# Summing the keys of the self attention before the row-sum matmuls

## The reference, cut to what matters

```
def sdpa(q, k, v, causal):
    scale = 1.0 / np.sqrt(q.shape[-1])
    scores = jnp.einsum('bhqd,bhkd->bhqk', q * scale, k)
    if causal:
        mask = jnp.tril(jnp.ones((q.shape[-2], k.shape[-2]), dtype=bool))
        scores = jnp.where(mask, scores, jnp.finfo(jnp.float32).min)
    p = jax.nn.softmax(scores.astype(jnp.float32), axis=-1).astype(q.dtype)
    return jnp.einsum('bhqk,bhkd->bhqd', p, v)
```

## Time and profile before

| | us |
|---|---|
| median of 3 runs | 748.28 |
| the three runs | 746.57, 749.37, 748.28 |
| the profiled execution | 751.68 |
| its span | 749.9 |
| PE busy, of the span | 678.5 (90%) |
| DVE busy | 400.0 (53%) |
| ACT busy | 352.7 (47%) |
| POOL busy | 109.0 (15%) |

### The profile page before, as it was taken

How to read it: one execution, slowest core, us unless ns; L and a number is a source line. 1 busy time by engine, 2 the same in 40 slices (tenths; PEclk the granted TensorE clock), 3 DMA queues, 4 the chain that set the end, 5 groups by cost and what they waited for, 6 DMA issues and landing times.

```text
span 749.9 us, 13217 instructions
## 1 busy us (share of the span) xinstructions
PE 678.5 (90%) x5514; PEld 538.6 (72%) x5514; DVE 400.0 (53%) x805; ACT 352.7 (47%) x711; POOL 109.0 (15%) x140
## 2 busy tenths in 40 slices
PE   5997997879999999999889979979799989999995
PEld 4885765548897777778768767755598967776984
DVE  2739537555574555341455684383685374645315
ACT  4522452477352666553434225526473236575424
POOL 0100000480000332200001000007600004132000
PEclk9997999698999999999989969968899999999998
DMA  8132001022004000050400200000120400000000
GB/s 291 64 152 85 2 1 30 1 78 78 1 1 169 1 2 1 1 190 1 183 28 1 77 9 2 2 29 12 68 78 1 168 1 2 1 2 1 0 1 28
DMA packets 6843, 34.54 MB, mean 46 GB/s; under 512 B 1537, under 2 KB 3073, under 8 KB 5249
## 3 DMA queue, kind: packets, MB, share of 16 engines
q1 hardware_dynamic: 5344, 26.85, 9.7%
q10 hardware_dynamic: 1440, 6.86, 2.5%
HBM read 32.66 MB, written 1.05 MB: 45 GB/s over the span
## 4 chain that ended last, share of the span: by engine, by line
PE 75%; DVE 14%; ACT 7%; issue 2%; DMA 1%; POOL 1%; SPq 0%; DVEq 0%; ACTq 0%; POOLq 0%
PE ps_A L733 5%; PE ps_B L952 4%; PE ps_A L952 4%; PE ps_B L733 3%; PE ps_A L915 3%; PE ps_B L915 3%; PE ps_A L1029 3%; PE ps_B L1029 3%; PE ps_B L1079 2%; PE ps_A L1079 2%; PE ps_A L748 2%; PE ps_A L1108 2%; PE ps_B L748 2%; PE ps_A L1067 2%; PE ps_B L863 2%
## 5 line engine op out<-in xcount | busy, mean ns | idle before, releaser
L562 POOL TENSOR_TENSOR xv_A<-big_A 128x256 f32<-128x256 f32 x24 | 18.0, 756 | 215.8 <-ACT big_A L1386 113.6
L562 POOL TENSOR_TENSOR xv_B<-big_B 128x256 f32<-128x256 f32 x24 | 18.5, 776 | 205.2 <-ACT big_B L1386 102.8
L1726 DVE TENSOR_REDUCE max_B<-ps_B 128x2 f32<-128x512 f32 x64 | 40.4, 685 | 14.7 <-PE ps_B L878 9.7
L1726 DVE TENSOR_REDUCE max_A<-ps_A 128x2 f32<-128x512 f32 x64 | 40.0, 685 | 13.9 <-PE ps_A L878 7.2
L1203 ACT ACT_TABLE_LOAD x31 | 39.8, 1283 | 0.5
L733 PE MATMUL ps_A<-q_A,kz_A 128*128 128x256 f32 x264 | 36.8, 300 | 3.2 <-DVE q_A L1617 3.2
L733 PEld LDWEIGHTS ps_A<-q_A,kz_A 128*128 128x128 f32 x264 | 34.7, 203 | 4.9 <-DVE q_A L1617 3.4
L733 PE MATMUL ps_B<-q_B,kz_B 128*128 128x256 f32 x264 | 36.7, 299 | 1.1 <-DVE kz_B L1638 1.1
L733 PEld LDWEIGHTS ps_B<-q_B,kz_B 128*128 128x128 f32 x264 | 34.7, 203 | 2.7 <-issue 2.4
L915 PE MATMUL ps_A<-q_A,kz_A 64*128 64x256 f32 (+1 forms) x320 | 32.7, 317 | 3.7 <-ACT big_A L1390 2.2
L1390 ACT ACTIVATE big_B<-ps_B 128x384 f32<-128x384 f32 (+1 forms) x48 | 23.7, 543 | 23.8 <-PE ps_B L926 23.7
(11 more groups left out here) (413 smaller groups left out, 1651.5 us busy)
## 6 DMA issues: line engine op xcount, KB each, us to landing
ffn_w<-in_l1m SPq DMA_DIRECT2D x2, 3072.0 KB, 11.1
ffn_w<-in_l2f SPq DMA_DIRECT2D x2, 3072.0 KB, 10.3
attn_w<-in_l1a SPq DMA_DIRECT2D x2, 2048.0 KB, 9.2
v_B<-in_l1d ACTq DMA_DIRECT2D x2, 1408.0 KB, 6.8
v_A<-in_l1d ACTq DMA_DIRECT2D x2, 1408.0 KB, 6.4
attn_w<-in_l2q SPq DMA_DIRECT2D x2, 1024.0 KB, 5.1
attn_w<-in_l2q SPq DMA_DIRECT2D x4, 512.0 KB, 4.9
v_A<-in_gm SPq DMA_DIRECT2D x2, 512.0 KB, 5.8
```

Of the source, the lines that this page charges most:

```text
L562: nc.gpsimd.tensor_tensor(L.key_sums(a, i), p[:, 0:S], p[:, S:2 * S], ALU.add)\
L1726: last = nc.vector.tensor_reduce(mx[:, :, h], L.ps[:, h % 4, :].rearrange("p (q k) -> p q k", q=ST), AX.X, ALU.max)
```

## The change

POOL gets a fourth block of additions, for the self heads. It adds the kt = 1 weights of queries 128 to 255 to the kt = 0 weights of the same queries, over 128 columns, and writes the sum into the head's unused first 128 columns. PE then takes the sums of a self head as two matmuls of 128 columns: the kt = 0 weights for queries 0 to 127, and the added tile for queries 128 to 255. That is 256 columns where there were 384. The number of matmuls and weight loads stays the same. Between the values and the sums of a self turn PE now waits on `halves_added`, and the semaphore's count per pass rises from 32 to 48.

All four `ORDER` lists are new. The parts that concern the self attention, read from the lists (sc n is `scores(n)`, W n is `weigh(n)`, what stands in brackets belongs to the other lane):

- PE, the last turn W3 before: lane B, it 0: sc 14, [turn_max], W3. Lane A, it 0: sc 14, [two cross maxima], W3. Lane A, it 1: sc 14, [sc 0], W3. Lane B, it 1: sc 14, [cross queries], W3.
- PE, the last turn W3 after: lane B, it 0: sc 14, [turn_max, sc 0], W3. Lane A, it 0: sc 14, [two cross maxima], W3. Lane A, it 1: sc 14, [sc 4, W0], W3. Lane B, it 1: sc 14, [two steps of self dense], W3.
- POOL after: 16 self adds of B then 16 of A in it 0; 12 of A, 2 of B, 2 of A, 2 of B, 2 of A, 12 of B in it 1. The clearing of both lanes' value buffers (line 571) stands ahead of them in both passes.
- The order of the two lanes also changes in the cross attention of both batches, in the second latent block of it 0, in the second gated memory layer of it 0 and the first of it 1 (lane B now goes first), and in the experts' part of it 1. ACT starts lane B's load of the down weights later (behind lane A's first cross exponentials).

```
 ORDER = {
     "PE": [
         0, 1, 2, 1, 1, 1, 2, 3, 2, 1, 1, 2, 4, 2, 3, 8, 5, 1, 2, 1, 1, 5, 1, 3, 1, 1, 1, 1, 2, 1, 2, 3, 2,
-        3, 1, 3, 1, 2, 1, 1, 1, 4, 2, 1, 2, 1, 1, 1, 1, 2, 2, 1, 1, 2, 2, 2, 5, 1, 1, 1, 1, 1, 1, 1, 2, 2,
+        3, 1, 3, 2, 2, 1, 5, 3, 1, 3, 1, 2, 1, 1, 2, 2, 2, 5, 2, 1, 2, 1, 1, 1, 1, 2, 1, 1, 1, 1, 1, 2, 2,
...
     "POOL": [
-        0, 1, 1, 1, 1, 16, 16, 8, 8, 9, 10, 1, 13, 1, 1, 1, 2, 14, 6, 2, 2, 6, 8, 8],
+        1, 2, 1, 16, 16, 13, 2, 1, 4, 1, 4, 1, 6, 8, 8, 8, 1, 1, 8, 1, 13, 2, 2, 2, 2, 12, 9, 1, 1, 2, 1, 1,
+        3, 4, 2, 8, 6, 2, 2, 6, 8, 8],
...
-                self.halves_added = s("halves_added", 32)
+                self.halves_added = s("halves_added", 48)
...
-                        nc.gpsimd.tensor_tensor(L.key_sums(a, i), p[:, 0:S], p[:, S:2 * S], ALU.add)\
-                            .then_inc(L.halves_added.sem, 1)
+                        if a == SELF:
+                            add = nc.gpsimd.tensor_tensor(p[:, 0:P], p[:, P:S], p[:, S + P:2 * S], ALU.add)
+                        else:
+                            add = nc.gpsimd.tensor_tensor(L.key_sums(a, i), p[:, 0:S], p[:, S:2 * S], ALU.add)
+                        add.then_inc(L.halves_added.sem, 1)
                         yield
...
-                for block in (1, 2, 3):
+                for block in range(4):
                     yield from add_halves(L, block)
...
-                        for part in range(2 if a == SELF else 1):
-                            for kt in range(ST):
-                                lo = kt * P if a == SELF else 0
-                                for j in range(tiles):
-                                    h = order[b * tiles + j]
-                                    at = (1 - kt) * S
-                                    last = mm(strip(j, part, lo), sums(a, h) if part else L.values(a, h, kt),
-                                              L.weights(a, b * tiles + j)[:, at + lo:at + S],
-                                              start=(first and part == 0 and kt == 0),
-                                              stop=(a == SELF and final and part == 1 and kt == ST - 1),
-                                              skip_group_check=True)
-                        if a != SELF:
-                            pe.wait_ge(*L.halves_added.at(it, n0 - HEADS + (b + 1) * tiles))
+                        for kt in range(ST):
+                            lo = kt * P if a == SELF else 0
                             for j in range(tiles):
-                                last = mm(strip(j, 1, 0), sums(a, order[b * tiles + j]), L.key_sums(a, b * tiles + j),
-                                          start=False, stop=final, skip_group_check=True)
+                                at = (1 - kt) * S
+                                mm(strip(j, 0, lo), L.values(a, order[b * tiles + j], kt),
+                                   L.weights(a, b * tiles + j)[:, at + lo:at + S],
+                                   start=(first and kt == 0), stop=False, skip_group_check=True)
+                        pe.wait_ge(*L.halves_added.at(it, n0 + (b + 1) * tiles))
+                        for half in range(2 if a == SELF else 1):
+                            for j in range(tiles):
+                                i = b * tiles + j
+                                if a == SELF:
+                                    p = L.weights(a, i)[:, 0:P] if half else L.weights(a, i)[:, S:S + P]
+                                else:
+                                    p = L.key_sums(a, i)
+                                last = mm(strip(j, 1, half * P)[:, 0:P] if a == SELF else strip(j, 1, 0), sums(a, order[i]), p,
+                                          start=False, stop=(final and half == (a == SELF)), skip_group_check=True)
                         last.then_inc(L.pv_done.sem, 1)
```

## The result

The change made the kernel slower: 752.28 us (median of 9 runs, 751.78 to 754.63) against 746.57 (9 runs of before beside them, 745.11 to 750.00). The ratio is 1.0072, 95% interval 1.0049 to 1.0096, so +5.4 us on 747. The profiled execution took 754.63, its span is 752.8, 2.9 us more than the span before. Both executions were long ones for their kernel: 754.63 is the longest of the nine, and the 751.68 of before is longer than all nine beside it.

A forecast was written before the change was run, and what follows sets the result against it. The prediction took PE to bound the kernel (busy 678.5 of 749.9 us). The profiled 751.68 us, less 3.4, plus 0.9, with wait and order at 0, gave 749.2, or 745.8 on the median's level; range 740 to 752.

The forecast's parts named there:

- What bounds the kernel: Whole kernel: PE, busy 678.5 of 749.9 us and 75% of the chain, sets the pace, also in the self stages.
- the shorter sums on PE: Self attention turns: sums take 0.44 instead of 0.65 us, 0.21 saved in each of 16 turns, 3.4 us in all.
- The added wait: PE between values and sums of a self turn: adds of 0.41 us finish in time, cost 0, at worst 1.2 us.
- 64 adds on POOL: Self stages: POOL's adds hidden, but they meet 14 DVE operations and cost 0.9 us, between 0 and 5.7.
- Rival D: Self stage: POOL and DVE lock each other out and adds come late, +6.1 us, giving 754.4; chance 0.16.
- The new order of steps: Outside the self stage: neighbouring steps of the two lanes exchanged, cost taken as 0, bounds -4.4 to +4.4 us.
- Rival C: Stages behind the self attention wait for DVE's maxima, so the end doesn't see the saving: 748.3 us; chance 0.14.
- Rival B: Cross stages: the new order also cuts PE's idle time by a fifth, 22 to under 19 us, giving 741.4; chance 0.22.
- The signs named for a wrong forecast: Self stages not shorter, or more than 3 us arising or vanishing in stages that compute the same as before.

The follow-up runs named there:

- e1: The edit (self adds, PE's wait, shorter sums) with all steps in the order of before: 745.50 us, ratio 0.9972 to the kernel before.
- e4: Kernel before, old order, with two sums of 128 columns per self head but no adds and no wait: 749.21 us, ratio 0.9989.
- e3: Kernel before, old order, with POOL's self adds and PE's wait, but sums still over 384 columns: 749.84 us, ratio 1.0002.
- e2: Kernel before with the new order of steps on all engines and without the edit: 761.41 us, ratio 1.0169.
- e13: e6 plus the new order in the second half of it 0's latent attention and its feed-forward: 746.81 us, ratio 0.9962 to before.
- e9: e6 plus the new order in the first part of it 0's latent attention: 745.78 us, ratio 0.9955 to before.
- e6: The edit in the order of before, except it 0's start up to lane B's cross scores 12 in the new order: 744.88 us, ratio 0.9943 to before.
- e11: The changed kernel with the end of it 0's cross attention put back to the old order: 752.32 us, ratio 1.0045 to before.
- e10: e6 with lane B's last cross turn, dense and sum of squares of it 0 later on PE, ACT's B steps too: 756.60 us, ratio 1.0112 to before.
- e8: The edit in the order of before, except from lane A's second cross maximum of it 1 to the end, new: 753.30 us, ratio 1.0068 to before.
- e7: The edit in the order of before, except B's eighth up-projection (it 0) to A's second cross maximum (it 1), new: 756.07 us, ratio 1.0110 to before.
- e15: The changed kernel with the gated stages and projections between the iterations put back to the old order: 755.66 us, ratio 1.0100 to before.
- e12: The changed kernel with it 0's cross end and everything from A's second cross maximum of it 1 put back to old: 751.36 us, ratio 1.0040 to before.

## Why the prediction was wrong

*What bounds the kernel, and the shorter sums on PE: right.* A turn on the chain is 1.23 us, as forecast, and the self stage of it 0 is 66.5 - 64.8 = 1.7 us shorter in e1 and e4. That is 8 turns at 0.21, half of the 3.4. (In the new order the whole edit is worth 1.0%, over which part of the lost clock falls too; no term of the sum has that.)

*The added wait: right at 0.* The add was mis-sized, 0.457 and not 0.41 us: a line through two clearings gave POOL's fixed part as 0.10 us, while the two adds (0.727 for 256 columns, 0.457 for 128) make it 0.19. Nothing waited for it all the same.

*64 adds on POOL: 0.9 us forecast, not seen.* e3 has all the adds and the wait and none of the saving, and its ratio is 1.0002. Three adds and one DVE operation of the self stages were stretched, where the term had 14 meetings at a chance of 0.3 each. Rival D had the sign of the result and nearly the size (754.4), by luck: its mechanism did not happen.

*The new order of steps: this is the step that failed.* "Its cost isn't in any row ... a fifth of it won or lost, -4.4 to +4.4. I take 0." The order costs 12.6 us without the edit (e2) and 7.5 us with it, so both the value and the bound were wrong. It accounts for nearly all of the miss: -2.5 was forecast and +5.4 measured, 7.9 us apart. The bound was worked out from PE's idle time in the cross stages, as if the order could only fill or widen those gaps. It left out two things. First, the gated stages, where PE is busy for about 10 of 15 us and the two lanes were swapped (2.0 us with the self stage behind them). Second, the clock. Whole stretches are at 1.2 GHz, and a bound on idle time doesn't hold for what they cost. One lies at 172 to 179 us in the changed kernel, behind the gaps of 3.37 and 1.64 on PE, as if the gaps had brought it on. But e13, with the old cross end and no gap over 1.1 us there, has a stretch of the same length, with PE busy throughout (first row e13; then the changed kernel):

```profile
165.00:172.00 7.00, 7.00 (x40) 6.11 (x32) 1.45 (x2) 1.09 (x2) 3.45 (x4) 0.51 0.01 2
172.00:179.00 7.00, 5.61 (x27) 5.61 (x28) 6.85 (x11) 1.86 (x5) 0.00 (x0) 0.52 0.01 2
```

Before and e9 have it too, e6 and e11 don't. So it is not shown that the new order's gaps bring on slow stretches.

Part of the material for a signed estimate was there. The lists said that B's last cross turn of it 0 moved behind twelve more of A's heads, and the trace of before had the length of the chain from that turn to the up-projection. A look at what fills PE during that chain would have given the sign. It would hardly have given the size: with that look in hand I expected 3 to 5 us of e10, and it was 16.

*Rival C* (the end doesn't see the saving) is half true for single executions: e1 gains 1.7 us in the self stage, and in its profiled execution loses it to the clock right behind. Over 12 runs 2.5 us remain. *Rival B* is wrong for the cross stages (28.5 us idle, not under 19). But some of the new order gains: the start, with A's first scores ahead of B's last self turn, gives another 1.7 us in the self stage (63.1 against 64.8).

The signs named for a wrong forecast held: "if more than 3 us arise or vanish in stages that compute the same as before".

What stays open is what decides between the two lengths of the slow clock with the same steps (e1 and e8, e7 and e8), and so how the 7.5 us divide between the order itself and the clock. Estimates can be had where stages have the same lost clock in two traces. The start is -1.7 us (e6 against e1) and the latent stage -1.6 (e13 against e6). The cross end of it 0 is about +2.6: 90.8 in the changed kernel and e15, against 88.0 and 88.3 in e9 and e13, all with 11.9 lost; the other half of the 5 us between the changed kernel and e11 goes with the clock, 11.9 against 8.5. The gated stages with the self stage behind them are +2.0. Together these are 1.3 us. The cross end of it 1 is longer too, 145.6 in e8 and 144.1 in e11 against 138.5, with 5 and 9 us more of lost clock. At the same 15.4 us lost, e8's 145.6 stand against e12's 142.0, but the stages in front differ. So 3.6 us is an estimate of the most that is the order's own there, and what is left of the 7.5 goes with the clock.

The version to keep is e6, the edit with the start alone in the new order: 0.9943 of before (0.9912 to 0.9975), about 4 us faster than before and 1.3% faster than the changed kernel. That it is faster than the edit in the old order (e1) shows in the self stage of the traces, not in the ratios.

## What to carry to other kernels

When a change brings a new order of steps with it, treat the order as the larger change: find each lane's longest chain over the engines between two big blocks of PE work, and see in both orders what PE does meanwhile. A step moved behind the other lane's work delays everything that hangs on it, and the work that would have covered the chain is done before the chain starts. Test an edit and its order apart. Don't add up prices of stretches of an order, since what one stretch does changes the clock and the start of the next. Where the order swaps two lanes, cut the trace where both are through, or the swap itself looks like a loss.

## What the runs showed of the hardware

I had not expected that the same steps differ by 6 us in one stage with the granted clock alone: down at 125 us, and up again at 138 in e8 and at 157 in e7, on one chip. In one program it shows in the times. Of the twelve runs of e1, nine lie between 741.2 and 746.1 us with a mean granted clock of 0.940 to 0.948, and three between 749.6 and 751.9 with 0.930 to 0.934. Of 29 runs of the kernel before that stood beside e1 to e4, 13 lie between 744.9 and 746.8 us, 15 between 748.1 and 751.7, and one at 755.0. So a median of three or even nine runs moves by several microseconds without any change in the program: that of before is 746.57 over the nine runs beside the changed kernel, and from 747.3 to 750.8 over the 23 to 29 runs on each of the four chips of the experiments. Only runs on the same chip, side by side, can be compared, and the stages of two profiles tell more than two medians, if they are compared at the same lost clock.
